# Stacking projection tiles of eight neighbouring heads one by one, instead of pairs of tiles with alternating heads

## The reference

```python
q = einsum('bhtr,hrd->bhtd', einsum('btd,hdr->bhtr', xn, q_a), q_b)   # 16 heads, rank 64, head size 16
k = ... the same with k_a, k_b
v = xn @ v_w.T + v_b
att = softmax(causal(q @ k^T / 4));  y = att @ v;  attention = y @ o_w.T + o_b
# experts: 8 experts, each takes its top 128 tokens of every batch by gate,
# silu(x_in @ w1[e]) @ w2[e], scaled by the gate, added back at the token's row
```

## Time and profile before

| | us |
|---|---|
| median of 3 runs | 1244.37 (1242.15 to 1245.09) |
| profiled execution, its own time | 1248.95 |
| profiled execution, its span | 1247.2 |
| PE busy | 1163.1 (93%) |
| DVE busy | 1013.3 (81%) |
| ACT busy | 682.7 (55%) |
| POOL busy | 702.6 (56%) |

### The profile page before, as it was taken

The page is one execution under the profiler, slowest core; times in us unless marked ns, Lnnn a source line. Parts: engine busy times, 40 slices in busy tenths (PEclk is TensorE's granted clock), DMA queues, the critical chain, the costliest instruction groups (busy, mean ns, idle before and its releaser), DMA issues. The chain is left out here.

```text
span 1247.2 us, 26009 instructions
## 1 busy us (share of the span) xinstructions
PE 1163.1 (93%) x8508; PEld 812.9 (65%) x8508; DVE 1013.3 (81%) x3396; ACT 682.7 (55%) x1330; POOL 702.6 (56%) x1021
## 2 busy tenths in 40 slices
PE   6789999999999999999999998869999999999994
PEld 5535556556556555555555554448989999999994
DVE  3589988988889999999999988679967676777762
ACT  2347777777677676676676666543423243333330
POOL 1235354354354354354354366754888888888875
PEclk9779999999999999999999999889999999999997
DMA  7552553553453552552551644224666666566654
GB/s 146 119 120 71 135 121 88 135 120 94 129 120 91 133 120 79 130 134 66 140 132 58 149 113 131 65 72 115 127 126 120 113 125 136 112 114 141 107 77 46
DMA packets 112730, 139.39 MB, mean 112 GB/s; under 512 B 21836, under 2 KB 79828, under 8 KB 112596
## 3 DMA queue, kind: packets, MB, share of 16 engines
q1 hardware_dynamic: 82756, 102.84, 32.3%
q0 software_dynamic: 24576, 33.57, 16.2%
q10 hardware_dynamic: 5264, 1.32, 0.6%
HBM read 53.22 MB, written 33.55 MB: 70 GB/s over the span
## 5 line engine op out<-in xcount | busy, mean ns | idle before, releaser
L808 DVE CUSTOM_DVE_ANT_0 junk<-bank,rowmask 128x256 bf16<-128x256 f32 (+3 forms) x1024 | 446.7, 482 | 48.9 <-PE bank L958 44.9
L660 ACT ACTIVATE probs<-bank 128x512 f32<-128x512 f32 x640 | 365.9, 596 | 134.1 <-PE bank L979 127.3
L560 POOL TENSOR_SCALAR_AFFINE_SELECT probs<-probs 128x256 f32<-128x256 f32 (+1 forms) x640 | 229.3, 372 | 255.7 <-ACT probs L660 252.4
L958 PE MATMUL bank<-kstk,qstk 96*128 96x256 bf16 (+3 forms) x1024 | 249.6, 305 | 14.0 <-DMA kstk<-qk_part 7.7
L979 PE MATMUL bank<-qstk,kstk 98*128 98x256 bf16 (+3 forms) x1024 | 250.0, 306 | 11.8 <-DMA qstk<-maxrow 9.7
L1142 POOL DMA_INDIRECT out_rows<-mixed,rows x128 | 212.1, 1657 | 58.3 <-issue 37.5
L1000 PE MATMUL bank<-probs,vaug 128*32 128x512 f32 (+3 forms) x2048 | 179.7, 446 | 5.0 <-POOL probs L560 5.0
L979 PEld LDWEIGHTS bank<-qstk,kstk 98*128 98x128 bf16 x1024 | 76.3, 98 | 148.3 <-ACT probs L660 91.7
L1166 ACT ACTIVATE hid<-bank 128x512 f32<-128x512 f32 x128 | 76.4, 598 | 172.3 <-PE bank L1259 146.6
L1277 PE MATMUL bank<-w_hi,hid_hi 128*128 128x256 f32 x512 | 147.3, 288 | 0.0
L1277 PE MATMUL bank<-w_hi,hid_lo 128*128 128x256 f32 x512 | 144.9, 283 | 0.0
(11 more groups left out here) (149 smaller groups left out, 2171.7 us busy)
## 6 DMA issues: line engine op xcount, KB each, us to landing
qstk<-qk_part SPq DMA_DIRECT2D x96, 256.0 KB, 5.1
kstk<-qk_part SPq DMA_DIRECT2D x96, 256.0 KB, 5.0
qstk<-in_L_ffn_w SPq DMA_DIRECT2D x32, 512.0 KB
xln<-in_L_attn_hidden_states SPq DMA_DIRECT2D x16, 512.0 KB, 6.7
xn_rows<-xn SPq DMA_DIRECT2D x16, 512.0 KB, 2.9
xres<-in_L_attn_hidden_states SPq DMA_DIRECT2D x16, 512.0 KB, 4.0
out_rows<-xres SPq DMA_DIRECT2D x16, 512.0 KB
out_rows<-mixed,rows POOLq DMA_INDIRECT x128
```

The costliest lines, as they stand in the source:

```text
L560: nc.gpsimd.affine_select(out=block, in_=block, compare_op=ALU.is_ge, fill=0.0, base=0, pattern=[[0, len(cols)], [1, P]], channel_multipli ...
L660: nc.scalar.activation(probs[n % 2][:, 512 * k:512 * k + 512], SCORET[k % 2][:], ACT.Exp, scale=SCALE).then_inc(exp_done, 1)
L808: last = nc.vector.tensor_tensor_reduce(out=junk[k % 2][:, col:col + width], in0=SCORE[score_bank(UN * n + k)][:, col:col + width], in1=ro ...
L958: last = nc.tensor.matmul(SCORE[score_bank(UN * n + k)][:, col:col + width], qstk[b % 2][0:KS, GH * g + h, P * i:P * i + P], kstk[b % 2][0 ...
```

## The change

The folded weights' columns are written so that tile m of a pair holds heads 8m to 8m + 7, not every second head. Each tile can then be stacked by itself: after every `mid` step (k = 0, 1, 2, 3) SP issues six DMAs of 128 KB, with 1 KB per source partition, into half of the stack's heads. A batch has 24 of these DMAs. The wait for the stack to be free (`scoret_ready`) moves from `mid` 1 to `mid` 0.

```diff
-            STACK_DMAS = 16 * 2 * len(TERMS)
+            STACK_DMAS = 16 * 4 * len(TERMS)
...
-                        elif kind == "mid" and k % 2 == 1:
-
-                            if n >= 2 and k == 1:
+                        elif kind == "mid":
+
+                            if n >= 2 and k == 0:
                                 sp.wait_ge(scoret_ready, at(UN * GB * (n - 1), 8 * UN))
                                 sp.sem_inc(sp_past, 1)
                             sp.wait_ge(lo_done, at(GB * n + k + 1, 2 * GB))
-                            side = k // 2
+                            side, m = divmod(k, 2)
                             stk = (qstk, kstk)[side][n % 2]
                             for t, term in enumerate(TERMS):
-                                sp.dma_start(stk[t:KS:len(TERMS), :, :],
-                                             qk_part[term[side]][:, 2 * side:2 * side + 2, :]).then_inc(stacked[n % 2], 16)
+                                sp.dma_start(stk[t:KS:len(TERMS), H // 2 * m:H // 2 * m + H // 2, :],
+                                             qk_part[term[side]][:, k, :]).then_inc(stacked[n % 2], 16)
...
-                                src[:, 0:D].rearrange("p (h m j) -> p m h j", m=2, h=8), ACT.Copy).then_inc(hi_done, 1)
+                                src[:, 0:D].rearrange("p (m h j) -> p m h j", m=2, h=8), ACT.Copy).then_inc(hi_done, 1)
...
-                                     src[:, 0:D].rearrange("p (h m j) -> p m h j", m=2, h=8),
+                                     src[:, 0:D].rearrange("p (m h j) -> p m h j", m=2, h=8),
```

## The result

The changed kernel takes 1236.42 us (median of 6 runs, 1232.49 to 1238.19) against 1244.14 of before: a ratio of 0.9938, interval 0.9923 to 0.9953. The forecast was 1238.4. The profiled execution of the changed kernel took 1236.28 us.

A forecast was written before the change was run, and what follows sets the result against it. TensorE paces up to 399 us; then DVE, also ranking gates, is nearly full. Terms 5.1 + 1.0 + 1.0 + 0.4 - 0.6 = 6.9 us, taken as 6: 1244.4 - 6 = 1238.4 us, range 1232 to 1254.

The forecast's parts named there:

- The mechanism of a burst: Stack DMAs: six of 256 KB take 9.1 us, limited by DMA engines; afterwards 0.66 us issues run beside 0.65 us transfers.
- Price of a packet: Stack DMAs between SBUF tiles: 1 KB packets cost 73 to 84 ns, about half of 147 ns for 2 KB.
- packets cost more than their bytes: Rival on stack DMAs: at 100 ns a packet the stack lands 1.1 us later in 14 batches, 1258 us; chance 10%.
- The stack ready 0.9 us earlier: Steady batches, slot 1: k stack lands 0.9 us earlier (0 to 1.5), worth 5.1 us in early batches, 1.0 in late.
- The load of x: Issued between k halves, landing in 4.5 us: 0.4 us late in six batches, on time in others, costing 0.6 us.
- this rival: The load of x still takes 6.4 us to land, costing 16 us in all: 1254 us; chance 13%.
- The waits on the maxima: TensorE at slot 1 waits 4.5 us early, 0.5 later for the 8 KB DMA, which would meet less backlog.
- Prologue: First k burst: last DMA lands at 52.9 us against 53.3, a gain of 0.4 us.
- The last stacking: Batch 15, with no load of x between its halves: its slot waits 1.9 us, of which 1.0 us is gained.
- Column order: Fold evictions read columns in one run; ACT's four take 2.5 us, bounding the gain; nothing was taken.
- ACT's issue pushing in: Where ACT's DMA issue interrupts the k burst, the stack lands up to 0.8 us later before the change.
- The signs that I named: 192 issues near 600 ns; last landings near 3 us; packets near 75 ns; slot 1 waits under 4 us; L746 under 1.

The follow-up runs named there:

- the kernel with x ahead: Changed kernel with the load of x issued ahead of both k halves instead of between them: 1234.03 us (0.9896 to before), again 1229.93 us (0.9885).
- x behind both: Changed kernel with the load of x issued behind both k halves, some 4 us later: 1279.14 us, 1.0275 to before.
- the k side alone: Changed kernel with only the k side new, the q side keeping its old head order and 256 KB DMAs: 1246.95 us, 1.0010 to before.
- small DMAs issued late: Changed kernel with each side's twelve 128 KB DMAs issued only when its second tile is done: 1262.61 us, 1.0129 to before.

## Why the prediction was right, and where its terms were off

- **Direction and size**: 6 us forecast, 7.7 measured, within the range. The mechanism of a burst, six DMAs limited by transfer against twelve limited by issue, is borne out where nothing else is in the queue. But the sum is right in part by luck: its largest term, 5.1 us from an earlier stack in the early batches, stood for a stack that came hardly earlier, and what filled its place were the waits on the maxima.
- **Price of a packet**: taken as 73 to 84 ns. For a burst that runs by itself that was too dear. The q1 row of the first burst of the changed kernel, 33 to 43 us, beside the earlier trace rows, and that of the kernel with x ahead, second profile, 176 to 180 us:

```profile
q1 hardware_dynamic: 1728, 1.57, 57.1%
...
q1 hardware_dynamic: 993, 0.90, 112.3%
```

  0.571 x 10 x 16 us / 1728 = 52.9 ns a packet; with 19 to 20 ns for each of 192 completion packets, 57 ns for 1 KB, less than half of the 147 ns for 2 KB. The second row is a k burst stacked up behind x, with the engines full: 1.123 x 4 x 16 us / 993 = 72 ns a packet, and with 20 ns for each of its some 110 completion packets 79 ns for 1 KB. That is half of the 147 ns, inside the forecast's bounds. So the price goes by bytes when the queue is full, and is lower when it isn't. The rival "packets cost more than their bytes" falls. Issues cost 602 ns at the median, as forecast.
- **The stack ready 0.9 us earlier**: the step that was off most. From T + 12.4 it went to 12.1, in the second profile to 12.3 (means over the seven batches that can be read): 0.1 to 0.3 us. I had added x's transfer to the sum, 1.5 us, and took the landing as T + 11.4 by transfers; measured, x in between costs the second half 2.1 us (against x behind both), so what was left out is a delay beyond the transfer, read above as x's latency. With x ahead of both halves the stack lands at T + 10.9, 1.5 us earlier than before.
- **The load of x**: I forecast 0.4 us late in six batches and 0.6 us of cost. It was late in 12 of 13, by 0.7 us at the mean (8.6/13), for it took 5.0 us to land at the median where I took 4.5. With x ahead 6.6 us come back, from this wait and from the stack together. So this rival was real but smaller than its 16 us: at the median, landing stayed under the 5.3 us from which I said it decides, though it was over it in 6 of the 13 steady loads (5.5 to 6.4 us).
- **The waits on the maxima**: counted in the forecast only where the k stack waits too. They went almost everywhere. Three of them, 2.5 us in all, lay before T of batch 2 (at 73.19, 82.53 and 125.15 us), and the sum had nothing for them. The two rows of the table before T of batch 2 give 0.8 + 1.6 us, where the sum had 0.4 for the prologue. This made up for the steady batches, 566.05 to 562.44, that is 3.6 us (2.5 in the second profile) for 5.1 + 1.0 - 0.6 forecast.
- **Prologue**: the first score unit waited 1.2 us where it had waited 2.2, and started at 53.86, 8.5 us after the fourth low part in place of 9.3: 0.8 us for the 0.4 forecast. That it stands later on the clock is the late arrival of the weights.
- **The last stacking**: its wait of 1.9 us is gone (0.2 left in its stretch). I took 1.0 us; the last rows of the table hold it, but one profile of each can't part it from the rest.
- **Column order**: no gain, as taken. L613's four take 633 ns still.
- **ACT's issue pushing in**: wrong as the cause of 0.8 us. The q burst at 165.55 us of before overlaps an ACT issue and lasts 4.18 us, its longest issue 922 ns: 0.2 to 0.3 us over the burst at 44.15, which overlaps none. The long bursts hold a packet of an instruction queue, below. The L958 at 562.01 that the forecast read as ACT's doing stands behind such a burst.
- **The signs that I named**: two came, 192 issues a stack near 600 ns each, and a wait of DVE's L746 under 1 us a batch at the mean, though it was over 1 us in three batches. Three didn't: the last landing near 3 us (4.9 in the batch shown), the q1 packets near 75 ns in a burst that runs by itself (53), and TensorE's waits at slot 1 under 4 us (6.5). They missed on the x load and on the price, as above.

What stays open: why DVE waits longer for x with the k side alone (13.5 us) than with both (9.8); what ACT's stall is, seen in five of ten profiles with and without the change; and what the 2.4 us of the last row are.

## What to carry to other kernels

Split a burst of transfers that ends just before its reader so that the first part goes while the second is still made; but count the issues, for here twelve short DMAs ended no sooner than six long ones when all started together. Look at what else stands in the issuing queue between the parts: here one load that changed its place was worth almost as much as the change. Look for small urgent DMAs on other queues: here the long bursts held one up too. And when an experiment makes TensorE wait longer, look at its granted clock before the loss is put down to the wait.

## What was not expected of the hardware

**SP's own instructions.** In bursts of six issues that last over 4.5 us one or two single issues are long, and a packet group of an instruction queue, mostly "q8 instruction", falls into the burst. The burst of before at 118.77 us, DMA packets by queue and the line view:

```profile
q1 hardware_dynamic: 504, 0.94, 74.7%
q8 instruction: 1, 0.02, 1.5%
...
L477 SPq DMA_DIRECT2D qstk<-qk_part x6: 552/603/1653, 118.8 to 122.3; - x6
```

One issue took 1653 ns where 603 is usual. The burst at 128.9 has no q8 packet and its longest issue is 738 ns. In the trace of before twelve of these issues take over 1.1 us: nine have a q8 packet beside them, two one of the other instruction queue, q14, one has none. In the changed kernel all thirteen have a q8 packet. Such packets also fall beside issues of the usual length. That the fetch of instructions holds up the issue is argued from this, not shown by a run.

**The price of a packet is no constant.** 2 KB between SBUF tiles cost 147 ns with the engines full; 1 KB cost 79 ns with them full and 57 ns with them at a share of 0.6 to 0.8.

**A longer wait was followed by a lower clock.** Behind a wait of 3.07 us TensorE ran at 1.2 GHz for 6.9 us, with small DMAs issued late. In the steady part of before, where its waits at slot 1 are 1.3 us a batch at most, the clock stays at 1.00.
